# Attention's denominators: the row sums of both query halves in four products of 32 columns, one reciprocal a round, spread over the partitions by ScalarE

## The chip, the cores and the metric

One core of a Trainium2 chip runs the whole program. TensorE (PE in the rows) multiplies, VectorE (DVE), ScalarE (ACT) and GpSimd (POOL) do the rest, and each engine takes its instructions strictly in the order written, waiting on semaphores. The metric is the time of one execution on the device in microseconds. Three runs of the kernel before took 1800.47 to 1801.7 us, median 1801.14.

## The reference

Four layers over x of 4 batches x 1024 tokens x 128 features: attention with 16 heads of 64, experts, a linear attention, experts again, each on a layer norm and added to x. The change is in the first:

```python
s = jnp.einsum('bhid,bhjd->bhij', q * scale, k)
gm = jax.lax.stop_gradient(jnp.max(s, axis=-1, keepdims=True))
p = jnp.where(causal_mask, 0.0, jnp.exp(s - gm))
num = jnp.einsum('bhij,bhjd->bhid', p, v)
out = num / (jnp.sum(p, axis=-1, keepdims=True) + EPS)
```

## The kernel before

Attention takes the first 1245 us. It works in 32 rounds, one for each pair of heads of each batch, and each round has two stages, t = 0 and t = 1. The query rows come in two halves of 512: index n = 0 is the upper half (tokens 512 to 1023, eight parts of keys), n = 1 the lower one (four parts). In round r TensorE makes the scores of round r + 1 (only for their row maxima, which VectorE takes), then the same scores again, turned and shifted by the maximum, for round r. ScalarE exponentiates these tiles into `prob`, POOL masks the diagonal blocks and adds the tiles of a half up into `row_sum[n]`, and TensorE multiplies them by the values into the bank `pv`. Score tiles and shifted tiles share a ring of three banks, so a tile can be written when the one three places before it has been read; `STAGES` writes their order out by hand.

The denominators go through a bank of their own, `alone`, which the turned maxima use too. `sums(p, n)` (L1389 to L1394) multiplies `row_sum[n]` of each head by 64 columns of ones, so each sum stands on all 64 partitions of its head. `denominator` (L1051) copies it out with a small constant added, `inverse` (L1176) takes the reciprocal in two pieces of 128x256 in place, and POOL's `normal` (L935) multiplies the values' product `o[n]` by it. Half n = 0 of round p has its sums at the end of round p, stage 1; half n = 1 has them in stage 0 of round p + 1. The reciprocals of half 0 stand behind VectorE's maxima in stage 0 of round p + 1, those of half 1 in its stage 1; POOL's normalising products follow in stage 1 and in stage 0 of round p + 2.

ScalarE's list at the end of stage 1 is: the tiles, `rows` (the maxima for the next shifts), `high` twice (the next round's projections), then `product_out` (L1046, the copy of `pv`) and `denominator`, and then the next round's tiles. TensorE ends an odd round with `outwards` (L1412), the output projection of two head pairs, which waits for POOL's normalised halves and starts with the rows of half 0; VectorE adds the result to x. In the last round and the two behind it there are no scores for a next round; the first expert weights are split and the first routing is worked out there.

## Time and profile before

| | |
|---|---|
| Median of three runs | 1801.14 us |
| The profiled execution, whole | 1801.88 us |
| Its span | 1800.1 us |
| Busy: PE, DVE, POOL, ACT | 1725.6, 1421.9, 1309.2, 1027.8 us |
| Reciprocals of the denominators (L1179) | 128, 214.7 us busy |
| Copies of the denominators (L1054) | 64, 44.0 us busy |
| Sums' matmuls (L1393), records | 256 |

Busy times are of the whole span. A product of plain 32-bit operands stands as two records in the trace, its two passes. A record's length holds the latency too: the next one starts before it ends, so what a product costs is read from start to start. The trace's span begins and ends with the first and last instruction; 1.8 us lie around it.

### The profile page before, as it was taken

The page shows a single profiled execution, that of the slowest core. Times are in us where ns is not written, and L with a number is a line of the kernel's source. Part 1 is how long each engine was busy: PE and PEld are TensorE (multiplying, and loading weights), DVE is VectorE, ACT ScalarE, POOL GpSimd, SP SyncE. Part 2 cuts the span into 40 slices and gives each one's busy share as a digit, 9 for nine tenths or more (in the row PEclk, how much of TensorE's full clock was granted, in tenths as well). Part 3 has the DMA queues.
Part 4 walks back from the last instruction along what each step waited for, and adds up shares of the span by engine and source line. Part 5 has one row for each costly group of instructions (what it writes and reads, how often), then busy time and mean ns, then how long its engine had stood idle before and what let it go on. Part 6 is the DMA issues. An engine that isn't in the chain of part 4 may idle for free. (4 is left out here: it accounts for less than half of the span.)

```text
span 1800.1 us, 32515 instructions
## 1 busy us (share of the span) xinstructions
PE 1725.6 (96%) x11638; PEld 1263.0 (70%) x11638; DVE 1421.9 (79%) x2459; ACT 1027.8 (57%) x2177; POOL 1309.2 (73%) x1354
## 2 busy tenths in 40 slices
PE   6999999999999999999999999998999979889998
PEld 4767677677776777777777767766888756568786
DVE  6778778787787887777777777765999958979887
ACT  3555444455445444545544445453889876649876
POOL 1777767677686776777667676776899957738998
PEclk9999999999999999999999999998999989989999
DMA  3000000000000000000000000001000000000000
GB/s 95 2 1 1 1 1 1 1 1 1 1 1 2 1 1 1 1 1 1 2 1 1 2 1 1 1 24 32 1 1 1 1 1 1 1 1 7 13 13 18
DMA packets 15088, 10.86 MB, mean 6 GB/s; under 512 B 433, under 2 KB 14546, under 8 KB 14930
## 3 DMA queue, kind: packets, MB, share of 16 engines
q1 hardware_dynamic: 14930, 8.80, 1.7%
q8 instruction: 94, 1.54, 0.3%
q14 instruction: 64, 0.52, 0.1%
HBM read 6.70 MB, written 2.10 MB: 5 GB/s over the span
## 5 line engine op out<-in xcount | busy, mean ns | idle before, releaser
L1160 DVE TENSOR_REDUCE attn_neg<-attn_shared 128x2 f32<-128x1024 f32 x512 | 611.8, 1223 | 250.1 <-PE attn_shared L1340 248.9
L1022 ACT ACTIVATE attn_prob<-attn_shared 128x1024 f32<-128x1024 f32 x288 | 295.1, 1026 | 368.3 <-PE attn_shared L1367 368.2
L924 POOL TENSOR_TENSOR attn_row_sum<-attn_row_sum,attn_prob 128x1024 f32<-128x1024 f32 (+3 forms) x256 | 418.2, 1634 | 24.2
L312 ACT ACTIVATE experts_weighed<-experts_y,kept_gate 128x128 f32<-128x128 f32 x1024 | 278.7, 410 | 50.1 <-PE experts_y L559 42.3
L901 POOL TENSOR_TENSOR attn_prob<-attn_prob,attn_below 128x256 f32<-128x256 f32 x256 | 188.3, 736 | 127.2 <-ACT attn_prob L1022 127.1
L405 DVE SCALAR_TENSOR_TENSOR experts_acc<-experts_y,kept_gate,experts_acc 128x128 f32<-128x128 f32 x896 | 247.2, 342 | 23.0 <-PE experts_y L559 20.6
L919 POOL TENSOR_TENSOR attn_row_sum<-attn_prob 128x1024 f32<-128x1024 f32 x64 | 135.6, 2118 | 162.4 <-ACT attn_prob L1022 159.9
L1336 PE MATMUL attn_shared<-attn_qk_hi 64*128 64x512 f32 x1024 | 232.9, 429 | 8.5 <-DVE attn_qk_lo L1173 2.9
L1340 PE MATMUL attn_shared<-attn_qk_hi,attn_qk_lo 64*128 64x512 f32 x1024 | 215.7, 392 | 0.0
L1179 DVE RECIPROCAL attn_den<-attn_den 128x256 f32<-128x256 f32 x128 | 214.7, 1719 | 0.3 <-ACT attn_den L1054 0.3
L1338 PE MATMUL attn_shared<-attn_qk_lo,attn_qk_hi 64*128 64x512 f32 x1024 | 214.5, 390 | 0.0
L557 PE MATMUL experts_y<-kept_w_hi,kept_xT_hi 128*128 128x512 f32 x512 | 206.0, 402 | 4.0 <-PEq L725 2.1
L558 PE MATMUL experts_y<-kept_w_lo,kept_xT_hi 128*128 128x512 f32 x512 | 202.1, 395 | 0.0
L559 PE MATMUL experts_y<-kept_w_hi,kept_xT_lo 128*128 128x512 f32 x512 | 201.6, 394 | 0.0
L1336 PEld LDWEIGHTS attn_shared<-attn_qk_hi 64*128 64x128 f32 x1024 | 107.4, 184 | 105.2 <-issue 84.8
L233 POOL TENSOR_TENSOR experts_quad_sum<-experts_quad_sum,experts_weighed 128x512 f32<-128x512 f32 x128 | 161.7, 1294 | 4.4 <-ACT experts_weighed L312 4.4
L1049 ACT ACTIVATE attn_o<-attn_pv 128x512 f32<-128x512 f32 x64 | 38.2, 598 | 211.7 <-PE attn_pv L1385 205.8
L1367 PE MATMUL attn_shared<-attn_neg_rows,attn_pick 64*128 64x512 f32 (+3 forms) x768 | 143.5, 344 | 0.0
L1365 PE MATMUL attn_shared<-attn_qk_hi,attn_qk_lo 64*128 64x512 f32 (+3 forms) x768 | 142.8, 342 | 0.0
L1363 PE MATMUL attn_shared<-attn_qk_lo,attn_qk_hi 64*128 64x512 f32 (+3 forms) x768 | 142.3, 342 | 0.0
L1361 PE MATMUL attn_shared<-attn_qk_hi 64*128 64x512 f32 (+3 forms) x768 | 139.7, 335 | 0.0
L1385 PE MATMUL attn_pv<-attn_prob,attn_v 128*64 128x512 f32 (+3 forms) x768 | 134.2, 490 | 2.3 <-POOL attn_prob L901 2.3
(263 smaller groups left out, 3345.3 us busy)
## 6 DMA issues: line engine op xcount, KB each, us to landing
kept_x<-in_L_attn_a_x_dram SPq DMA_DIRECT2D x4, 512.0 KB, 8.6
kept_half_raw<-_ffn_expert_weights_dram SPq DMA_DIRECT2D x4, 512.0 KB, 4.6
out_dram<-kept_x SPq DMA_DIRECT2D x8, 256.0 KB, 2.3
attn_prob<-in_L_attn_a_Wkv_dram SPq DMA_DIRECT2D x2, 512.0 KB, 6.1
attn_prob<-in_L_attn_a_Wq_dram SPq DMA_DIRECT2D x1, 512.0 KB, 4.9
attn_wo<-in_L_attn_a_Wo_dram SPq DMA_DIRECT2D x1, 512.0 KB, 5.7
attn_bo<-in_L_attn_a_bo_dram SPq DMA_DIRECT2D x1, 64.0 KB, 5.8
linear_weights_raw<-in_L_attn_b_Wg_dram SPq DMA_DIRECT2D x1, 64.0 KB
```

What stands on the lines that cost most here:

```text
L312: ins = act.activation(weighed[n][:, e, :], y[fill(pair, quad, odd) % RING][:, e * D:(e + 1) * D], ACT.Copy, scale=k.gate[:, c, quad * PER ...
L405: dve.scalar_tensor_tensor(out=to, in0=y[fill(pair, quad, odd) % RING][:, e * D:(e + 1) * D], scalar=k.gate[:, c, quad * PER + e:quad * PE ...
L557: pe.matmul(y[n % RING][:, :], k.xT_hi[:, at], hi, start=True, stop=False)
L558: pe.matmul(y[n % RING][:, :], k.xT_hi[:, at], lo, start=False, stop=False)
L559: pe.matmul(y[n % RING][:, :], k.xT_lo[:, at], hi, start=False, stop=True).then_inc(mm_ok, 1)
L924: pool.tensor_tensor(row_sum[n][:, :, at:], row_sum[n][:, :, at:], src, ALU.add).then_inc(add_ok, 1)
L1022: act.activation(prob[n % RING][:, :, :], buffer((p, t))[:, :, :], ACT.Exp).then_inc(exp_ok, 1)
L1160: dve.tensor_reduce(neg[p % 2][:, :, b, half], buffer((p, b, half))[:, :, :], AX.X, ALU.max, negate=True).then_inc(max_ok, 1)
L1179: dve.reciprocal(den[n][:, at], den[n][:, at]).then_inc(inv_ok, 1)
L1336: pe.matmul(buffer(u)[:, h, :], hi[head(h), 0, rows], hi[head(h), 1, at], start=True, stop=False)
L1338: pe.matmul(buffer(u)[:, h, :], hi[head(h), 0, rows], lo[head(h), 1, at], start=False, stop=False)
L1340: ins = pe.matmul(buffer(u)[:, h, :], lo[head(h), 0, rows], hi[head(h), 1, at], start=False, stop=True)
```

## The change

The sums of a round are taken once, in stage 0 of the next round: four products of 32 columns of ones, one for each head and half, put the four sums on four quadrants of 32 partitions of `alone`. One `denominator` and one `inverse` of two pieces (in stage 1) serve them all. Then `spread`, on ScalarE in stage 1 ahead of `product_out`, copies the quadrants to where the normalising products need them: four copies of 32x512 into `den[1]`, a wait for them, and two within `den[0]`. POOL's two normalising products both stand in stage 0 of round p + 2. `row_sum` and `o` of half 0 get a second buffer; room for it comes from `qk_lo`, whose second buffer now lies in `k.w_lo`, so the last two splits of expert weights wait for the last shifted tile.

```diff
         if valid(r):
             single.append(("turned", r, 1))
         if valid(r - 1):
-            single.append(("sum", r - 1, 1))
+            single.append(("sum", r - 1, 0))
         if valid(r + 1):
             single.append(("turned", r + 1, 0))
-        if valid(r):
-            single.append(("sum", r, 0))
     place = {u: n for n, u in enumerate(shared)}
     earlier = {u: single[n - 1] if n else None for n, u in enumerate(single)}
 
...
-        qk_lo = [sb(f"qk_lo{i}", [P, 2, N], F32R) for i in range(2)]
+        qk_lo = [sb("qk_lo0", [P, 2, N], F32R), k.w_lo[:, 16:32, :].rearrange("p (m x) d -> p m (x d)", m=2)]
...
-        row_sum = [sb(f"row_sum{n}", [P, 2, HALF]) for n in range(2)]
+        row_sum = [[sb(f"row_sum0_{i}", [P, 2, HALF]) for i in range(2)], [sb("row_sum1", [P, 2, HALF])]]
...
-        o = [sb(f"o{n}", [P, HALF]) for n in range(2)]
+        o = [[sb(f"o0_{i}", [P, HALF]) for i in range(2)], [sb("o1", [P, HALF])]]
...
+        def quadrant(h, n):
+            return slice(QUADRANT * (2 * h + n), QUADRANT * (2 * h + n + 1))
...
                 if i in (0, 8):
-                    need(pool, sum_ok, 2 * (p - 1) + n + 1)
+                    need(pool, sum_ok, p if n else p - 1)
...
 
             def normal(p, n):
 
-                pool.wait_ge(inv_ok, PIECES * (2 * p + n + 1))
+                pool.wait_ge(spread_ok, p + 1)
                 pool.wait_ge(o_ok, 2 * p + n + 1)
                 need(pool, out_ok, (p - 3) // 2 + 1)
-                pool.tensor_tensor(o_norm[p % 3][:, at_half(1 - n)], o[n][:, :], den[n][:, :], ALU.mult).then_inc(norm_ok, 1)
+                pool.tensor_tensor(o_norm[p % 3][:, at_half(1 - n)], product_of(p, n)[:, :], den[n][:, :], ALU.mult).then_inc(norm_ok, 1)
 
             for r in range(FIRST, LAST):
                 for t in range(STEPS):
...
                     if t == 1 and valid(r + 1):
                         cut(r + 1, 0)
                     if t == 0 and valid(r - 2):
+                        normal(r - 2, 0)
                         normal(r - 2, 1)
-                    if t == 1 and valid(r - 1):
-                        normal(r - 1, 0)
                     if (r, t) == (END + 1, 0):
                         pool.wait_ge(first_step, TOPPED)
                         pool.tensor_tensor(weights, weights, wide(top), ALU.subtract).then_inc(first_step, 1)
...
 
             def product_out(p, n):
                 act.wait_ge(pv_ok, UNITS * p + (UNITS if n else 8))
-                need(act, norm_ok, 2 * (p - 1) + n + 1)
-                act.activation(o[n][:, :], pv[:, :], ACT.Copy).then_inc(o_ok, 1)
-
-            def denominator(p, n):
-                act.wait_ge(sum_ok, 2 * p + n + 1)
-                need(act, norm_ok, 2 * (p - 1) + n + 1)
-                act.activation(den[n][:, :], alone[:, :], ACT.Identity, bias=sum_eps[:, :], scale=1.0).then_inc(den_ok, 1)
+                need(act, norm_ok, 2 * p if n else 2 * (p - 2) + 1)
+                act.activation(product_of(p, n)[:, :], pv[:, :], ACT.Copy).then_inc(o_ok, 1)
+
+            def denominator(p):
+                act.wait_ge(sum_ok, p + 1)
+                need(act, norm_ok, 2 * p)
+                act.activation(den[0][:, :], alone[:, :], ACT.Identity, bias=sum_eps[:, :], scale=1.0).then_inc(den_ok, 1)
+
+            def spread(p):
+
+                act.wait_ge(inv_ok, PIECES * (p + 1))
+                for h in range(2):
+                    for n in range(2):
+                        act.activation(den[1][quadrant(h, n), :], den[0][quadrant(h, 1), :], ACT.Copy).then_inc(moved_ok, 1)
+                act.wait_ge(moved_ok, 4 * (p + 1))
+                for h in range(2):
+                    ins = act.activation(den[0][quadrant(h, 1), :], den[0][quadrant(h, 0), :], ACT.Copy)
+                ins.then_inc(spread_ok, 1)
 
             for r in range(FIRST, LAST):
                 for t in range(STEPS):
...
                         if job_at(r, 3) is not None:
                             turned_high(job_at(r, 3))
                         if valid(r - 1):
-                            denominator(r - 1, 1)
+                            denominator(r - 1)
                         if r == END:
                             act.wait_ge(first_step, TURNED_ROUTER)
                             act.activation(k.rT[:, 0, :], router_bank(), ACT.Copy).then_inc(first_step, 1)
...
                         if valid(r + 2):
                             high(r + 2, 0)
                             high(r + 2, 1)
+                        if valid(r - 1):
+                            spread(r - 1)
                         if valid(r):
                             product_out(r, 0)
-                            denominator(r, 0)
                         if r == END:
                             act.wait_ge(first_step, LOGITS)
                             act.activation(weights, first_logits(0), ACT.Copy).then_inc(first_step, 1)
...
                 dve.tensor_tensor(qk_lo[p % 2][:, :, at], buffer(("qk", p, n))[:, :, :], f(qk_hi[p % 2][:, :, at]),
                                   ALU.subtract).then_inc(lo_ok, 1)
 
-            def inverse(p, n, piece):
+            def inverse(p, piece):
                 at = slice(piece * HALF // PIECES, (piece + 1) * HALF // PIECES)
-                dve.wait_ge(den_ok, 2 * p + n + 1)
-                dve.reciprocal(den[n][:, at], den[n][:, at]).then_inc(inv_ok, 1)
+                dve.wait_ge(den_ok, p + 1)
+                dve.reciprocal(den[0][:, at], den[0][:, at]).then_inc(inv_ok, 1)
 
             def into_x(g):
                 c = g // 4 * BLOCKS
...
             def expert_low(q):
                 dve.wait_ge(w_rounded, q + 1)
                 dve.wait_ge(value_ok, ROUNDS)
+                if q >= 2:
+                    dve.wait_ge(shift_ok, len(TILES) * ROUNDS)
                 dve.tensor_tensor(k.w_lo[:, expert_piece(q), :], raw_piece(q), f(k.w_hi[:, expert_piece(q), :]),
                                   ALU.subtract).then_inc(w_split, 1)
 
...
                         maximum(*u)
                     if valid(r + 1):
                         smallest(r + 1, t)
-                    if valid(r - 1):
+                    if t == 1 and valid(r - 1):
                         for piece in range(PIECES):
-                            inverse(r - 1, t, piece)
+                            inverse(r - 1, piece)
                     if t == 0 and job_at(r, 0) is not None:
                         statistics(job_at(r, 0))
                     if t == 1 and job_at(r, 1) is not None:
...
                                     start=(j == 0), stop=(i in (7, 11)))
                 ins.then_inc(pv_ok, 1)
 
-            def sums(p, n):
-                alone_free(("sum", p, n))
-                pe.wait_ge(add_ok, ADDS * p + (11 if n else 7))
+            def sums(p):
+
+                alone_free(("sum", p, 0))
+                pe.wait_ge(add_ok, ADDS * (p + 1))
                 for h in range(2):
-                    ins = pe.matmul(alone[head(h), :], ones[:, :], row_sum[n][:, h, :], start=True, stop=True)
+                    for n in range(2):
+                        ins = pe.matmul(alone[quadrant(h, n), :], ones[:, :], row_sums(p, n)[:, h, :], start=True, stop=True)
                 ins.then_inc(sum_ok, 1)
 
             def turn_router():
...
                 if r == END:
                     turn_router()
                 if valid(r - 1):
-                    sums(r - 1, 1)
+                    sums(r - 1)
                 if valid(r):
                     for i in range(0, 3):
                         product(r, i)
...
                 if valid(r):
                     for i in range(3, 8):
                         product(r, i)
-                    sums(r, 0)
             pe.wait_ge(x_ok, ROUNDS // 2)
 
 
```

`attn_pv` is the bank of the values' product, `attn_alone` that of the sums, `attn_shared` the ring of score tiles. TensorE before, at the end of a round's stage 1:

```order
L1385 MATMUL attn_pv<-attn_prob0,attn_v1 64x256 [waits attn_mask_ok]
L1385 MATMUL attn_pv<-attn_prob0,attn_v1 64x256
L1393 MATMUL attn_alone<-attn_row_sum0,attn_ones 64x512 [waits attn_add_ok,attn_rows_ok]
L1393 MATMUL attn_alone<-attn_row_sum0,attn_ones 64x512
L1336 MATMUL attn_shared0<-attn_qk_hi0 128x512 [waits attn_max_ok,attn_lo_ok]
```

The same place after:

```order
L1406 MATMUL attn_pv<-attn_prob0,attn_v1 64x512 [waits attn_mask_ok]
L1406 MATMUL attn_pv<-attn_prob0,attn_v1 64x512
L1406 MATMUL attn_pv<-attn_prob1,attn_v1 64x256 [waits attn_mask_ok]
L1406 MATMUL attn_pv<-attn_prob1,attn_v1 64x256
L1357 MATMUL attn_shared2<-attn_qk_hi1 128x512 [waits attn_lo_ok]
```

Nothing stands there between the values' product and the scores. TensorE before, stage 0 of a round (values of the next pair, the sums of half 1, the values' product):

```order
L1322 MATMUL attn_shared1<-kept_w_lo,kept_xT_lo 128x256
L1323 MATMUL attn_shared1<-kept_w_lo,kept_xT_hi 128x256
L1393 MATMUL attn_alone<-attn_row_sum1,attn_ones 64x512 [waits attn_add_ok,attn_rows_ok]
L1393 MATMUL attn_alone<-attn_row_sum1,attn_ones 64x512
L1385 MATMUL attn_pv<-attn_prob6,attn_v1 64x512 [waits attn_exp_ok,attn_o_ok,attn_v_ok]
```

The same place after:

```order
L1344 MATMUL attn_shared2<-kept_w_lo,kept_xT_hi 128x256
L1416 MATMUL attn_alone<-attn_row_sum0_0,attn_ones 32x512 [waits attn_add_ok,attn_rows_ok]
L1416 MATMUL attn_alone<-attn_row_sum1,attn_ones 32x512
L1416 MATMUL attn_alone<-attn_row_sum0_0,attn_ones 32x512
L1416 MATMUL attn_alone<-attn_row_sum1,attn_ones 32x512
L1406 MATMUL attn_pv<-attn_prob5,kept_half_raw 64x512 [waits attn_exp_ok,attn_o_ok,attn_v_ok]
```

The two products of 64 columns have become four of 32, and they take both halves' row sums. ScalarE before, the end of stage 1 (maxima, projections, the values' product, the denominator, the next tiles):

```order
L1038 ACTIVATE attn_neg_rows<-attn_alone,attn_own_block 128x128 x4
L1026 ACTIVATE attn_qk_hi<-attn_shared 128x2x512 x2
L1049 ACTIVATE attn_o<-attn_pv 128x512
L1054 ACTIVATE attn_den<-attn_alone,attn_sum_eps 128x512
L1022 ACTIVATE attn_prob<-attn_shared 128x1024 x5
```

And after:

```order
L1045 ACTIVATE attn_neg_rows<-attn_alone,attn_own_block 128x128 x4
L1033 ACTIVATE attn_qk_hi<-attn_shared 128x2x512 x2
L1068 ACTIVATE attn_den<-attn_den 32x512 x4
L1071 ACTIVATE attn_den<-attn_den 32x512 x2
L1056 ACTIVATE attn_o_0<-attn_pv 128x512
L1029 ACTIVATE attn_prob<-attn_shared 128x1024 x5
```

The denominator is gone from there and six copies of `den` stand ahead of the values' product. On POOL the normalising product of half 0 moves from stage 1 to the start of the next stage 0, directly ahead of that of half 1.

## Rows read from the trace of the kernel before

**Rows 1.** table of stretches: us, busy (x instructions) by engine, then TensorE clock

```profile
core 0 of [0], span 1800.1 us
113.15:1168.17 1055.02, 1050.24 (x8170) 750.82 (x8168) 822.56 (x738) 512.93 (x741) 757.50 (x749) 1.00 0.00 1
1206.00:1234.20 28.20, 24.30 (x180) 14.16 (x177) 11.75 (x11) 11.90 (x19) 27.30 (x23) 0.97 0.14 39
```

**Rows 2.** waits, 100 to 1250 us: total us, times, longest

```profile
ACT attn_prob L1022 <- PE attn_shared L1367: 350.2, 266, 3.7
DVE attn_neg L1160 <- PE attn_shared L1340: 235.8, 293, 3.5
PE attn_shared L1336 <- DVE attn_neg L1160: 1.1, 7, 0.2
```

**Rows 3.** timeline of TensorE, end of round 17: start, us, line, names

```profile
708.98 3.73 PE L1423 MATMUL attn_shared<-attn_wo,attn_o_norm 128*128 128x128 f32 x32
715.71 1.03 PE L1393 MATMUL attn_alone<-attn_row_sum,attn_ones 128*64 128x512 f32 x4
```

**Rows 4.** timeline of TensorE, end of round 16 and next stage

```profile
676.37 1.03 PE L1393 MATMUL attn_alone<-attn_row_sum,attn_ones 128*64 128x512 f32 x4
677.33 0.50 PE L1336 MATMUL attn_shared<-attn_qk_hi 64*128 64x512 f32 x2
680.69 0.42 PE L1336 MATMUL attn_shared<-attn_qk_hi 64*128 64x512 f32 x2
```

**Rows 5.** timeline of TensorE's weight loads, sums of stage 0

```profile
617.19 0.20 PEld L1393 LDWEIGHTS attn_alone<-attn_row_sum,attn_ones 128*64 128x64 f32 x4 [0.17 <-issue]
```

**Rows 6.** timeline of VectorE, rounds 16 and 15

```profile
671.76 3.35 DVE L1179 RECIPROCAL attn_den<-attn_den 128x256 f32<-128x256 f32 x2
621.78 1.23 DVE L1160 TENSOR_REDUCE attn_neg<-attn_shared 128x2 f32<-128x1024 f32 x1 [2.16 <-PE attn_shared L1340]
```

**Rows 7.** timeline of ScalarE, 128x512 operations out of SBUF

```profile
1459.14 0.63 ACT L1658 ACTIVATE linear_gate<-linear_raw 128x512 f32<-128x512 f32 x1
1459.81 0.63 ACT L1660 ACTIVATE linear_gate<-linear_gate 128x512 f32<-128x512 f32 x1
1460.34 1.04 ACT L1661 ACTIVATE linear_log<-linear_raw 128x1024 f32<-128x1024 f32 x1
```

**Rows 8.** timeline of ScalarE, ends of rounds 16 and 17

```profile
679.29 1.03 ACT L1022 ACTIVATE attn_prob<-attn_shared 128x1024 f32<-128x1024 f32 x1 [1.15 <-PE attn_shared L1367]
715.92 0.60 ACT L1049 ACTIVATE attn_o<-attn_pv 128x512 f32<-128x512 f32 x1 [5.72 <-PE attn_pv L1385]
```

**Rows 9.** timeline of POOL, start of round 17

```profile
677.35 1.30 POOL L940 TENSOR_TENSOR attn_o_norm<-attn_o,attn_den 128x512 f32<-128x512 f32 x1
682.09 2.40 POOL L919 TENSOR_TENSOR attn_row_sum<-attn_prob 128x1024 f32<-128x1024 f32 x1 [3.45 <-ACT attn_prob L1022]
```

**Rows 10.** timelines of VectorE, POOL and TensorE, rounds 30 to 33

```profile
1199.28 3.35 DVE L1179 RECIPROCAL attn_den<-attn_den 128x256 f32<-128x256 f32 x2
...
1206.10 2.39 POOL L919 TENSOR_TENSOR attn_row_sum<-attn_prob 128x1024 f32<-128x1024 f32 x1
1219.26 1.27 POOL L940 TENSOR_TENSOR attn_o_norm<-attn_o,attn_den 128x512 f32<-128x512 f32 x1
1232.88 1.27 POOL L940 TENSOR_TENSOR attn_o_norm<-attn_o,attn_den 128x512 f32<-128x512 f32 x1
1239.83 1.26 POOL L940 TENSOR_TENSOR attn_o_norm<-attn_o,attn_den 128x512 f32<-128x512 f32 x1 [2.85 <-DVE attn_den L1179]
...
1235.88 3.61 PE L1423 MATMUL attn_shared<-attn_wo,attn_o_norm 128*128 128x128 f32 x16 [0.84 <-POOL attn_o_norm L940]
1241.15 2.05 PE L1423 MATMUL attn_shared<-attn_wo,attn_o_norm 128*128 128x128 f32 x16 [1.66 <-POOL attn_o_norm L940]
```

**Rows 11.** timeline of TensorE, round 15, two score units

```profile
625.33 0.43 PE L1340 MATMUL attn_shared<-attn_qk_hi,attn_qk_lo 64*128 64x512 f32 x2
625.91 0.51 PE L1336 MATMUL attn_shared<-attn_qk_hi 64*128 64x512 f32 x2
```

19 lines of the change are left out of this document (12 added, 7 removed).

## The prediction

> **What bounds the kernel now.** I read the table of stretches first. In the steady part of attention, 1055 of the 1800 us, TensorE is busy 1050.24 us of 1055.02 at full granted clock; VectorE works 822.56, GpSimd 757.50, ScalarE 512.93 us [rows 1]. The waits say the same from the other side: ScalarE spends 350.2 us waiting for the tiles it exponentiates, VectorE 235.8 us for the scores, and TensorE has 1.1 us of idle time put down to VectorE [rows 2]. So a microsecond taken from VectorE is worth nothing by itself, and one taken from TensorE's stream counts, if ScalarE and POOL can follow. After 1206 us this turns over: POOL is busy 27.30 of 28.20 us and TensorE 24.30 [rows 1]. That end is a chain of its own, read row by row at the end of the next part.
>
> Attention is 32 rounds (head pairs) of two stages. Rounds differ by parity: at the end of an odd one TensorE also does a projection outwards (3.73 us [rows 3]), at the end of an even one it does not. The 1055.02 us run from round 1's sums to round 29's, 28 rounds of 37.7 us; I work with round 16 (its sums at 676.37 us) and round 17 (715.71 us) and take the others of a parity for the same.
>
> **The change part by part.**
>
> *TensorE, end of stage 1: a pair of sums goes.* The four records of two products start within 1.03 us less one record's own duration and the scores follow 0.96 us after the first (677.33 - 676.37) [rows 4]. At the full array a record of 128 columns takes 3.73/32 = 0.117 us [rows 3], so four records of 512 columns one after another would stream about 1.8 us; they take 0.96 us with the change of shape to the 64-row scores behind them. So two column groups already work side by side, and the two passes of a product follow each other 0.43 us apart. Streaming is 0.86 us and the change of shape 0.10 us. The sum's 0.86 us goes; the change of shape stays, between the values' product and the scores.
>
> *TensorE, stage 0: two products of 64 columns become four of 32.* No row shows four column groups at once. Lower bound: all four stream together, 0.86 us as now, extra 0. Upper bound: two at a time as now, 1.72 us, extra 0.86 us. I take the lower, because the nearest rows show groups of different columns to be independent to within the resolution of the row, and both passes kept apart: nothing in them is shared but the rows, which are shared already. New beside it is a change of shape between 32 and 64 columns in front of the next values' product; the nearest is the 0.10 us above (bounds 0 and 0.2). So a round gains 0.86 - 0.10 = 0.76 us on TensorE.
>
> What a page would add here: the Trainium skill, "TensorEngine Tiling (Array Packing)", section Tiling Modes, lists four tiles of 128x32 that work independently, which is the lower bound. Against it stands the skill's "TensorE: Matmul & The Clock Gate", section The mechanism: weight loads overlap matmuls in flight only when the row group differs. Here the row group is the same, and the trace disagrees with it for 64 columns: four loads fall within 0.20 us from 617.19 on, while the matmuls that they belong to run for 0.9 us [rows 5]. By that rule the eight loads of a round, 0.14 us each, would stand in the open, 1.1 us a round and some 34 us in all; I keep it inside the first rival with 2 in 100.
>
> *VectorE.* Two reciprocals of 128x256 a round go, 3.35 us [rows 6], 31 times: 104 us of busy time. They stood in stage 0, behind the last maximum; in a round where VectorE had more to do there than usual it still idled 2.16 us before its next score at 621.78 us [rows 6]. That idle time covers them: worth 0. The pair in stage 1 stays where it was, ending at R = 671.76 + 3.35 = 675.11 us in round 16, and with it the low halves behind it.
>
> *ScalarE.* A 128x512 copy with bias goes from the end of stage 1. Six copies of 32x512 come in ahead of the copy of the values' product, and they wait for R. No row has 32 channels. The nearest are 128x512 operations: 0.63 us long, 0.53 us from one start to the next where it is independent (1459.81 to 1460.34), 0.67 us where it waits for the one before (1459.14 to 1459.81) [rows 7]. Lower bound: all at 0.53; upper: every one at 0.67. The program has one such wait, before the fifth copy: three steps of 0.53, one of 0.67, two of 0.53 make 3.32 us until the values' copy starts and about 0.5 us more until the first exponential (the values' copy lasts 0.60 us [rows 8] and overlaps its follower by 0.1, as those do). I add 0.04 us for the wake-up: the first exponential can start at R + 3.86 = 678.97 us.
>
> Even round: the scores now start at 677.33 - 0.86 = 676.47 us, and the third score unit, which takes the buffer that this exponential frees, moves from 680.69 to 679.83 us [rows 4]. The exponential began at 679.29 and ended at 680.32 before [rows 8]; now it ends at 680.00 and is seen a few hundredths later. TensorE stalls about 0.20 us. Later exponentials are spaced by TensorE's 1.63 us and take 1.03 us, so ScalarE catches up at once. Even round: gain 0.76 - 0.20 = 0.56 us. Odd round: ScalarE had idled 5.72 us in front of the values' copy at 715.92 us [rows 8]; 3.4 us of copies fit. Gain 0.76 us.
>
> *POOL.* Its two normalising products now stand together at the start of stage 0 and wait for the spread, which ends at R + 3.5 = 678.6 us; 1.3 us each, so they end at 681.2 us. The first row sum behind them began at 682.09 us after 3.45 us idle; with the 0.86 us gained it is due at 681.2 us, and a stall of ScalarE's moves it back by as much [rows 9]. It just fits; cost 0, and if the cover fails some tenths. The other buffers (second row sum, second product, alias of the low half) remove waits that no row shows: 0.
>
> *Body sum.* Rounds 0 to 29: 16 of them (15 odd ones and round 0, which has no spread yet) by 0.76 = 12.2 us, 14 by 0.56 = 7.8 us: 20.0 us gained.
>
> *The end, from round 30's stage 1.* Reciprocals end at 1199.28 + 3.35 = 1202.63 us. The spread ends 3.5 us later, 1206.1, and two products of 1.3 us bring POOL to 1208.7 us where it began the row sum at 1206.10: 2.6 us late, in the stretch where POOL never rests. The product at 1219.26 moves behind the sums; so the row sums end 1.3 us late, and the two products then end at 1236.8 us against 1234.15 [rows 10]: 2.6 us late. The last sum, its denominator and the reciprocals follow, 2.6 us late: they let POOL's last product go at 1239.83 before, now at 1242.4 us. But there the spread stands in between, to 1245.9 us, and two products behind it, the first to 1247.1. Only then can the outward projection start, of which the first half ran at 1235.88 before, under cover. At full clock its halves take 3.73/2 = 1.87 us and 2.05 us and end at 1251.1 us, against 1243.2: 7.9 us late. The first half ran 3.61 us before, at 1.2 GHz after TensorE had waited on POOL; if both halves do so, the end is about 11 us late. I take 9, between the two. The experts start behind this.
>
> *Total.* The profiled execution took 1801.88 us (span 1800.1 [rows 1] and 1.8 us around it), 0.7 us over the median of the runs. 1801.9 - 20.0 + 9 = 1790.9, and by the median's level 1790.2. I say 1790.5 us.
>
> **Rivals.**
>
> 1. *The four small products run two at a time* (ends on the other side). For it: the trace shows only two groups together. Against: they start as if independent. Price 0.86 us in each of 31 rounds, 26.7 us on TensorE: 1790.5 + 26.7 = 1817 us; half of it (three passes instead of two) gives 1804 us. It turns to slower from 0.46 us a round on. 17 in 100, with the weight-load rule in it.
>
> 2. *ScalarE gives the gain back.* Every copy steps at 0.67 us instead of 0.53, or POOL's pair misses its cover: 5 x 0.14 = 0.7 us more in 14 even rounds, 9.8 us: 1800 us, no change. For it: the slack in even rounds is used up to the last tenth. Against: independent operations overlap [rows 7]. 15 in 100.
>
> 3. *VectorE was a hidden bound.* TensorE's stream has small gaps between score units: from 625.33 to 625.91 us stand 0.58 us where a step of two products takes 0.23 us [rows 11]. If an earlier VectorE closed one such gap of 0.35 us a round, 30 rounds would give 10 us more: 1780 us. Against: VectorE waits before each such stage [rows 6]. 5 in 100. That the 104 us themselves come back is excluded by its 235.8 us of waiting.
>
> **How the numbers follow.** The forecast has 63 in 100. Its own bounds: no stall and no change of shape, 30 x 0.86 = 25.8 us gained less 7.9 at the end, gives 1783 us; a change of shape of 0.2 us, a stall of 0.4 and an end of 11 us give 1799 us. Rivals 1, 2 and 3 have 17, 15 and 5. The range 1783 to 1808 us leaves out the full price of rival 1 (about 12 in 100) and most of rival 3. A measurement here can tell 0.2%, 3.6 us, from no change. Faster: nearly all of the forecast, rival 3 and a little of rival 2, 67 in 100. Same: most of rival 2 and the half price of rival 1, 14. Slower: 19.
>
> **What the profile after would show.** Eight records of the sums within about 1.05 us, once a round (right), or within 1.9 us (rival 1). The copies starting 0.53 us apart, and the first exponential of an even round about 3.9 us after the reciprocals. From the end of round 16's scores stage to the end of round 17's 38.8 us, where 39.34 us stood between their sums [rows 3, 4]. VectorE busy 107 us less with TensorE's busy share in the body unchanged. POOL starting the last row sums 2.6 us after where the round would have them, and the last outward projection in one piece behind two products of POOL. The forecast is wrong if sums take over 1.3 us, if the first exponential stands over 4.5 us behind the reciprocals, or if the end costs less than 6 us or more than 13.

## The result, and the profile after

The changed kernel takes 1806.55 us (median of 8 runs, 1802.2 to 1808.55) beside 1801.18 us of the kernel before on the same chip (8 runs, 1799.7 to 1801.72): a ratio of 1.003, 95% interval 1.0019 to 1.004. It is slower by 0.3% where 0.6% faster was forecast. The range, 1783 to 1808 us, holds the time; the likeliest case does not.

The profiled execution took 1806.37 us, its span 1804.6 us. I read the table of stretches first, from round 1's sums to round 29's, the 28 rounds for which [rows 1] have 1055.02 us. In the changed kernel the sums stand only in stage 0, so the row of before is read again from there. Columns: from:to, us, then busy us (x instructions) of PE, PEld, DVE, ACT and POOL, then TensorE's granted clock, DMA share and GB/s. Before:

```profile
128.94:1183.97 1055.03, 1048.82 (x8157) 749.52 (x8157) 821.54 (x738) 511.39 (x737) 754.89 (x744) 1.00 0.01 1
```

After:

```profile
127.27:1176.64 1049.37, 1031.10 (x8156) 726.87 (x8157) 730.34 (x681) 596.25 (x877) 756.87 (x744) 1.00 0.01 1
```

Three columns did what they should: TensorE 18 us less busy, VectorE 91 us less, ScalarE 85 us more for 168 copies and 28 denominators less. But the 28 rounds are shorter by 5.66 us only, where the forecast had 18.5. TensorE was busy in all but 6.21 us of the stretch before and leaves 18.27 us open now. So the question is what it waits for, and the waits say it (engine line waited for: us in total, times, longest; TensorE, 100 to 1180 us):

```profile
PE attn_shared L1357 <- ACT attn_prob L1029: 11.0, 15, 0.8
PE attn_alone L1416 <- ACT attn_neg_rows L1045: 3.5, 12, 1.6
PE attn_shared L1357 <- DVE attn_neg L1179: 1.8, 11, 0.2
```

The first line is new against [rows 2]: in each of 15 rounds the third score unit waits for an exponential. The place is the end of an even round and the first scores behind it, where [rows 8] have the exponential at 679.29 us (an even round runs, in what follows, from the sums in its stage 0 to those in the next round's). The timelines of VectorE and ScalarE there (start, us, engine, line, names, shape, count, idle time before and who ended it):

```profile
667.49 3.35 DVE L1198 RECIPROCAL attn_den<-attn_den 128x256 f32<-128x256 f32 x2
...
670.88 2.59 ACT L1068 ACTIVATE attn_den<-attn_den 32x512 f32<-32x512 f32 x4 [0.70 <-DVE attn_den L1198]
673.49 1.27 ACT L1071 ACTIVATE attn_den<-attn_den 32x512 f32<-32x512 f32 x2
674.79 0.60 ACT L1056 ACTIVATE attn_o<-attn_pv 128x512 f32<-128x512 f32 x1
675.28 1.94 ACT L1029 ACTIVATE attn_prob<-attn_shared 128x1024 f32<-128x1024 f32 x2
```

and TensorE, which answers to 680.69 of [rows 4]:

```profile
675.32 0.40 PE L1388 MATMUL attn_shared<-attn_neg_rows,attn_pick 64*128 64x512 f32 x2
676.45 0.50 PE L1357 MATMUL attn_shared<-attn_qk_hi 64*128 64x512 f32 x2 [0.73 <-ACT attn_prob L1029]
```

R, the end of the reciprocals, is 667.49 + 3.35 = 670.84 us. The four copies start 0.65 us apart, the sixth is followed by the copy of the values' product (674.79) and this by two exponentials without a gap: ScalarE is late, and the first exponential starts at R + 4.44 us. It was put at R + 3.86. TensorE's step from 675.32 to 676.45 is 1.13 us where its neighbours are 0.23 apart, 0.90 us of waiting.

The sums themselves are fine. TensorE at round 16's sums, which now stand in stage 0 of round 17 (compare 677.33 of [rows 4] and the 715.71 of [rows 3]):

```profile
687.99 1.06 PE L1416 MATMUL attn_alone<-attn_row_sum,attn_ones 128*32 128x512 f32 x8
688.98 0.65 PE L1406 MATMUL attn_pv<-attn_prob,kept_half_raw 128*64 128x512 f32 x2
```

Eight records, four column groups in two passes, in the time in which four stood: the next product follows 0.996 us after the first of them, in every round. Before, the one behind the four records of stage 0 followed after 0.910.

The end, which answers to [rows 10] (POOL, ACT and PE of the last round):

```profile
1228.72 1.07 PE L1416 MATMUL attn_alone<-attn_row_sum,attn_ones 128*32 128x512 f32 x8
1241.77 6.49 PE L1446 MATMUL attn_shared<-attn_wo,attn_o_norm 128*128 128x128 f32 x32 [11.99 <-POOL attn_o_norm L948]
...
1236.41 2.58 ACT L1068 ACTIVATE attn_den<-attn_den 32x512 f32<-32x512 f32 x4 [1.93 <-DVE attn_den L1198]
1239.02 1.27 ACT L1071 ACTIVATE attn_den<-attn_den 32x512 f32<-32x512 f32 x2
...
1240.37 2.49 POOL L948 TENSOR_TENSOR attn_o_norm<-attn_o,attn_den 128x512 f32<-128x512 f32 x2 [6.76 <-ACT attn_den L1071]
```

```profile
1241.80:1248.20 6.40, 6.40 (x32) 6.27 (x32) 0.00 (x0) 0.00 (x0) 1.47 (x2) 0.56 0.00 0
```

TensorE waits 11.99 us, and then the outward projection runs in one piece at a granted clock of 0.56, near the lower of its two levels (1.2 GHz): 6.4 us instead of 3.73 [rows 3].

The budget, in the profiled executions' spans (divided at round 1's and round 29's sums in stage 0 and at the first weight load of the experts):

| piece, us | before | after | difference | forecast |
|---|---|---|---|---|
| up to round 1's sums | 128.94 | 127.27 | -1.7 | -1.5 |
| 28 rounds | 1055.03 | 1049.37 | -5.7 | -18.5 |
| round 29's sums to the experts | 61.27 | 73.42 | +12.2 | +9 |
| the rest | 554.84 | 554.52 | -0.3 | 0 |
| span | 1800.08 | 1804.58 | +4.5 | -11 |

Two terms failed, one by 12.8 us and one by 3.2 us.

### The profile page after: what moved, and what is told of

Its sections match the earlier page's. It is cut to its first block and busy times, and to the rows that moved or that the text cites. A ratio compares the mean times of both kernels' runs of the same rounds, so it can differ in the third digit from the quotient of the medians.

```text
span 1804.6 us, 32546 instructions
## 1 busy us (share of the span) xinstructions
PE 1706.2 (95%) x11638; PEld 1239.5 (69%) x11638; DVE 1317.4 (73%) x2395; ACT 1125.9 (62%) x2337; POOL 1309.5 (73%) x1354
## 5 line engine op out<-in xcount | busy, mean ns | idle before, releaser
L1406 PE MATMUL attn_pv<-attn_prob,kept_half_raw 128*64 128x512 f32 (+3 forms) x768 | 134.4, 492 | 0.0
L948 POOL TENSOR_TENSOR attn_o_norm<-attn_o,attn_den 128x512 f32<-128x512 f32 x64 | 80.8, 1284 | 55.2 <-ACT attn_den L1071 55.2
L557 PEld LDWEIGHTS experts_y<-kept_w_hi,kept_xT_hi 128*128 128x128 f32 x512 | 97.5, 190 | 28.4 <-DVE experts_acc L405 4.3
L559 PEld LDWEIGHTS experts_y<-kept_w_hi,kept_xT_lo 128*128 128x128 f32 x512 | 97.4, 190 | 21.3
L558 PEld LDWEIGHTS experts_y<-kept_w_lo,kept_xT_hi 128*128 128x128 f32 x512 | 97.5, 190 | 18.9
L1056 ACT ACTIVATE attn_o<-attn_pv 128x512 f32<-128x512 f32 x64 | 38.3, 598 | 111.8 <-PE attn_pv L1406 106.9
```

Of the source, the lines that this page charges most:

```text
L557: pe.matmul(y[n % RING][:, :], k.xT_hi[:, at], hi, start=True, stop=False)
L558: pe.matmul(y[n % RING][:, :], k.xT_hi[:, at], lo, start=False, stop=False)
L559: pe.matmul(y[n % RING][:, :], k.xT_lo[:, at], hi, start=False, stop=True).then_inc(mm_ok, 1)
L1406: ins = pe.matmul(pv[head(h), first:], v[g % 2][:, j, cols], slot(p, part)[:, h, place_of(part)], start=(j == 0), stop=(i in (7, 11)))
```

## The experiments

Theory A: ScalarE gives TensorE's gain back; the six copies take longer than the prediction had them, hold the first exponential of the next round, and stand in the chain at the end. Theory B: the 32-column products, or their place, cost TensorE more than they save. Theory C: VectorE or POOL, with their pair of normals, are the ones that are late.

**1. Without the copies.**

```
-                pool.wait_ge(spread_ok, p + 1)
+                pool.wait_ge(inv_ok, PIECES * (p + 1))
...
-                pool.tensor_tensor(o_norm[p % 3][:, at_half(1 - n)], product_of(p, n)[:, :], den[n][:, :], ALU.mult).then_inc(norm_ok, 1)
+                pool.tensor_tensor(o_norm[p % 3][:, at_half(1 - n)], product_of(p, n)[:, :], den[0][:, :], ALU.mult).then_inc(norm_ok, 1)
...
-                        if valid(r - 1):
-                            spread(r - 1)
```

> The changed kernel without the six spreading copies: the normals wait for the reciprocal alone and both halves multiply by the first denominator tile, so the denominators stay unspread and the attention output is another. Everything else stands as in the changed kernel. Theory A (ScalarE gives the gain back): the copies hold the first exponential of the next round until 4.48 us after the products of the sums instead of some 0.6 us, and TensorE waits for it 0.9 us in every even round. Without them the body gives the gain that was forecast (some 13 us more than it gave), and the copies ahead of rounds 30 and 31 go too, 3.9 us each at most: 1806.5 - 13 - 4 to 8 = 1782 to 1790, and the third score unit of even rounds waits less than 0.1 us. Theory B (the 32-column products or their place on TensorE cost more than they save): the copies lie beside other work, the waits before the score units stay, and only the last spread goes from the end: 1802 to 1804. Theory C (the loss is VectorE's or GpSimd's, the two normals side by side): the same as B.

Measured: 1782.52 us (4 runs, 1781.57 to 1784.38), ratio to before 0.9899 [0.9885, 0.9912]. The stretch of 28 rounds:

```profile
126.44:1160.33 1033.89, 1027.81 (x8156) 723.33 (x8156) 730.11 (x681) 492.14 (x709) 754.71 (x744) 1.00 0.01 1
```

1055.03 - 1033.89 = 21.14 us in 28 rounds, 0.755 us a round: the prediction's TensorE term was 0.76. By parity it is 35.73 to 34.97 us in even rounds (those without other work in them, as in all that follows) and 39.30 to 38.56 in odd ones. The wait for the exponential is gone:

```profile
PE attn_alone L1414 <- ACT attn_neg_rows L1045: 1.5, 1, 1.5
PE attn_shared L1355 <- DVE attn_neg L1177: 1.1, 7, 0.2
```

So B is wrong: the products, their shape and their place give all that they were said to. The copies cost 15.5 us in the 28 rounds: 14 x 1.0 us at the ends of even ones, and most of the rest in twelve rounds (nine odd ones of 38.67 us instead of 38.56, three even ones), in which TensorE waits some 0.12 us for ScalarE's rows of maxima (L1045: 3.5 us, 12 times, with the copies, 1.5 us, once, without). At the end 66.40 us stand between round 29's sums and the experts instead of 73.42: the copies are worth 7.0 us there. The other 5.1 us over the 61.27 of before stay without them: no run takes them apart. What is new there is the single sum and reciprocal, behind which both normals stand, and the projection that follows in one piece; without the copies it still takes 6.24 us, after 7.52 us of waiting.

**2 to 4. Fewer copies, and fewer of them ahead.** With five copies, one of 128x512 takes the whole reciprocal over first:

```
+                if step == 0:
+                    act.wait_ge(inv_ok, PIECES * (p + 1))
+                    act.activation(den[1][:, :], den[0][:, :], ACT.Copy).then_inc(moved_ok, 1)
+                    return
+                if step == 1:
+                    act.wait_ge(moved_ok, p + 1)
+                half, h = divmod(step - 1, 2)
+                ins = act.activation(den[half][quadrant(h, 1 - half), :], den[half][quadrant(h, half), :], ACT.Copy)
```

> The same result with five copies instead of six, all ahead of the copy of the values' product: one of 128x512 that takes the whole reciprocal into the second tile, then two of 32x512 in each tile. A normal waits for its own tile. Theory A: one step of 0.65 us goes from ahead of the first exponential, so up to 0.65 us of the 0.9 us stall in each of 14 even rounds (9 us), and the normal of the first half at the end may start two copies sooner: 1795 to 1800. Theories B and C: no change beyond 1 us, 1805 to 1807. The page should show the copies of 32x512 still 0.65 us apart; if a 128x512 copy ahead of them is followed after 0.53 us, it is the width, not the copies' kind, that keeps them from overlapping.

With four ahead, the last copies stand between the next round's exponentials, and POOL's normals behind its first addition:

```
+                    late = list(range(4, 6)) if t == 0 and valid(r - 2) else []
                     for p, i in turned_tiles(r, t):
                         exponential(p, i)
+                        if late:
+                            spread(r - 2, late.pop(0))
...
-                            spread(r - 1)
+                            for step in range(4):
+                                spread(r - 1, step)
```

> The same six copies, but only four of them ahead of the copy of the values' product; the last two follow the first and the second exponential of the next round, and GpSimd's two normals stand behind its first addition of that round instead of at its head. Theory A: the first exponential comes 1.31 us sooner, which is more than the stall of 0.9 us, so even rounds lose nothing there; the copies between the exponentials use time that ScalarE has: 14 x 0.85 = 12 us less, 1793 to 1798. If instead TensorE now waits for the second or third exponential, the gain is under half of it: 1800 to 1804. Theories B and C: 1805 to 1807.

And both together:

> Both edits: five copies, four of them ahead and the last one behind the first exponential, GpSimd's normals behind its first addition. Theory A: the first exponential as in the kernel with four ahead, with one copy of 0.65 us less between the later ones, and the end one or two copies shorter: 1791 to 1797, at or below the fastest of the other two correct ones and below the kernel before (1801). Theories B and C: 1805 to 1807.

Measured, each in 5 runs with the kernel before beside them (1800.49 us):

| kernel | us | ratio to before |
|---|---|---|
| five copies | 1795.47 (1789.43 to 1795.84) | 0.9958 [0.9945, 0.9972] |
| four of six ahead | 1792.89 (1791.76 to 1794.06) | 0.9955 [0.9942, 0.9967] |
| five, four of them ahead | 1790.52 (1787.13 to 1791.98) | 0.994 [0.9928, 0.9953] |

All three are faster than before and than the changed kernel, as A has it and B and C exclude; the last two came out just under the ranges expected (1793 and 1791 us). The 128x512 copy is followed after 0.66 us, but the copy behind it waits for it, so this says nothing on the width. ScalarE with four of six ahead, same place:

```profile
663.00 2.59 ACT L1074 ACTIVATE attn_den<-attn_den 32x512 f32<-32x512 f32 x4 [0.70 <-DVE attn_den L1210]
665.61 0.60 ACT L1059 ACTIVATE attn_o<-attn_pv 128x512 f32<-128x512 f32 x1
666.26 1.03 ACT L1032 ACTIVATE attn_prob<-attn_shared 128x1024 f32<-128x1024 f32 x1
667.32 0.63 ACT L1076 ACTIVATE attn_den<-attn_den 32x512 f32<-32x512 f32 x1
667.96 1.03 ACT L1032 ACTIVATE attn_prob<-attn_shared 128x1024 f32<-128x1024 f32 x1
```

The first exponential starts 3.26 us after the first copy instead of 4.40, and the two late copies cost nothing: the 28 rounds take 1035.43 us, 1.5 over the kernel without any copy. This edit moves POOL's normals too; experiment 8, which leaves them in their place, comes to the same length of the rounds. The one with five copies takes 1039.84 us, the one with both 1035.70.

**5. VectorE's half alone.** In the kernel before:

```
-                pool.wait_ge(inv_ok, PIECES * (2 * p + n + 1))
+                if n:
+                    pool.wait_ge(inv_ok, PIECES * (p + 1))
+                else:
+                    pool.wait_ge(den_ok, 2 * p + 1)
...
-                    if valid(r - 1):
+                    if t == 1 and valid(r - 1):
```

> The kernel before without VectorE's reciprocals of the first half of each round (62 instructions of 3.35 us, the half of VectorE's work that the change takes away): that half is multiplied by its denominator instead, so the output is another. The prediction put VectorE's saving at 0 us, because PE never waits for it in the rounds. By that, within 2 us of the kernel before, 1799 to 1803. By the rival that VectorE was a hidden bound, 7 us faster or more: under 1794.

Measured: 1800.77 us (11 runs) beside 1800.9 us (15 runs), ratio 1.0002 [0.9993, 1.0011]. (It is 64 instructions, 3.35 us a pair.) The stretch of [rows 1], from this kernel's own sums to sums:

```profile
112.05:1166.61 1054.56, 1049.71 (x8171) 746.78 (x8169) 731.21 (x682) 512.88 (x741) 756.97 (x749) 1.00 0.01 1
```

VectorE works 91 us less and the 28 rounds take 1054.56 instead of 1055.02 us, 0.02 us a round. The 104 us were worth nothing that the times show, as forecast, and rival 3, which had 10 us, is excluded.

**6 to 8. Why do the copies not overlap?** The step of 0.53 us in [rows 7] is 0.10 shorter than the operation; the copies' step of 0.65 is 0.02 longer. Three looks at the changed kernel, one run each. One increment for the four copies:

```
-                        act.activation(den[1][quadrant(h, n), :], den[0][quadrant(h, 1), :], ACT.Copy).then_inc(moved_ok, 1)
-                act.wait_ge(moved_ok, 4 * (p + 1))
+                        ins = act.activation(den[1][quadrant(h, n), :], den[0][quadrant(h, 1), :], ACT.Copy)
+                ins.then_inc(moved_ok, 1)
+                act.wait_ge(moved_ok, p + 1)
```

> The changed kernel with one semaphore increment behind the four copies instead of one behind each; the result is the same. Theory A1 (the increment closes the overlap: in the kernel with five copies and four ahead, the one copy without an increment is followed by the copy of the values' product after 0.54 us, where all that carry one take 0.65): the steps after the first three copies fall from 0.654 to about 0.54, the first exponential 0.3 us sooner. Theory A2 (32 partitions, or moving them, takes the overlap away): still 0.64 to 0.655 us.

Each copy to its own partitions:

```
-                        act.activation(den[1][quadrant(h, n), :], den[0][quadrant(h, 1), :], ACT.Copy).then_inc(moved_ok, 1)
+                        act.activation(den[1][quadrant(h, n), :], den[0][quadrant(h, n), :], ACT.Copy).then_inc(moved_ok, 1)
```

> The changed kernel in which the first four copies take each 32 partitions of the reciprocal to the same 32 partitions of the second tile, so nothing is moved across partitions and the second half is divided by other sums. Increments as in the changed kernel. If the move across partitions kept the copies apart, the step falls from 0.654 to about 0.53; if it is the 32 partitions or the increments, it stays at 0.65.

Two copies of 64 partitions for the four of 32:

```
-                    for n in range(2):
-                        act.activation(den[1][quadrant(h, n), :], den[0][quadrant(h, 1), :], ACT.Copy).then_inc(moved_ok, 1)
+                    act.activation(den[1][slice(64 * h, 64 * h + 64), :], den[0][slice(64 - 64 * h, 128 - 64 * h), :], ACT.Copy).then_inc(moved_ok, 1)
```

> The changed kernel in which two copies of 64x512, halves swapped, stand in the place of the first four of 32x512; the second half is divided by other sums. If a copy's time goes by its columns alone, each takes 0.63 us and is followed after 0.65; two steps go (1.3 us), and the first exponential comes at 3.2 us after the first copy instead of 4.4, before TensorE needs it: even rounds as without the spread, 35.0 us instead of 36.0. If a copy of 64 partitions takes longer, the gain is smaller by that.

Measured 1805.75, 1808.32 and 1788.45 us. ScalarE's rows, one kernel after the other:

```profile
671.66 2.55 ACT L1068 ACTIVATE attn_den<-attn_den 32x512 f32<-32x512 f32 x4 [0.70 <-DVE attn_den L1199]
```

```profile
671.73 2.59 ACT L1068 ACTIVATE attn_den<-attn_den 32x512 f32<-32x512 f32 x4 [0.72 <-DVE attn_den L1198]
```

```profile
664.43 1.28 ACT L1067 ACTIVATE attn_den<-attn_den 64x512 f32<-64x512 f32 x2 [0.70 <-DVE attn_den L1197]
665.75 1.27 ACT L1070 ACTIVATE attn_den<-attn_den 32x512 f32<-32x512 f32 x2
```

Four copies in 2.55, 2.59 and (two of them) 1.28 us. The increment is worth 0.013 us a copy (step 0.641 instead of 0.654), the move across partitions nothing, and the number of partitions nothing either: 64 take as long as 32 and as the 128 of experiment 2 (0.63 us). Theory A1, that the increments are the cause, is wrong: they are worth a hundredth, not a tenth. What all these copies share is that each stands next to one of 32 or 64 partitions; experiment 12 takes this up. Two copies fewer ahead do what nothing done to the single one does: the even rounds take 34.97 us, the length without copies, as expected.

**9. Another end** for the kernel with five copies, four ahead: in the last two rounds all ahead, in the last VectorE makes two of them.

```
+                            for step in range(4 if r < END else 5 if r == END else 3):
+                                spread(r - 1, step)
...
+                        if r - 1 == END:
+                            dve.wait_ge(moved_ok, ROUNDS)
+                            for h in range(2):
+                                ins = dve.tensor_copy(den[1][quadrant(h, 0), :], den[1][quadrant(h, 1), :])
+                            ins.then_inc(spread_ok, 1)
```

> The kernel with five copies, four ahead, with another end; the result is the same. In the last two rounds all copies of the reciprocal stand ahead, and in the last one VectorE makes the two copies of the second tile while ScalarE makes those of the first. Theory A: the body is as in that kernel (35.0 and 38.7 us between sums); the end loses one late copy in round 31 and the last normal two copies of 0.65 us: 1 to 2.5 us less, 1788 to 1790. If the end is bound by GpSimd's two normals one behind the other, nothing: 1790 to 1791.

Measured: 1789.48 us (5 runs, 1785.64 to 1790.68), ratio 0.9942 [0.9928, 0.9955] to the 1800.2 us beside it. From round 29's sums to the experts it takes 71.65 us where 72.95 stood: 1.3 us, inside the range expected, but too little to be told apart in the times from the 1790.52 us of the kernel without it. POOL in the last round:

```profile
1224.76 3.47 POOL L948 TENSOR_TENSOR attn_o_norm<-attn_o,attn_den 128x512 f32<-128x512 f32 x2 [4.81 <-ACT attn_den L1075]
```

The two normals stand one behind the other without a gap, so POOL is the next link. The first lasts 1.26 us and the second 2.25, beside VectorE's split of the expert weights; why is not tested.

**10 and 11. The place of the tile, and the kind of the instruction.**

```
-        den = [sb(f"den{n}", [P, HALF]) for n in range(2)]
+        den_first = sb("den0", [P, HALF])
...
+        den = [den_first, sb("den1", [P, HALF])]
```

> The changed kernel with the first denominator tile at another place of the on-chip memory, far from the second. Neither one increment less, nor no move across partitions, nor 64 partitions let the copies overlap; the copy of the values' product overlaps the next instruction by 0.10 us in the kernel before and ends 0.03 us ahead of it in the changed one, where only tiles have moved. If the places of the tiles decide, the steps of 0.654 us change here to about 0.53; if not, they stay.

```
-                        act.activation(den[1][quadrant(h, n), :], den[0][quadrant(h, 1), :], ACT.Copy).then_inc(moved_ok, 1)
+                        act.activation(den[1][quadrant(h, n), :], den[0][quadrant(h, 1), :], ACT.Identity,
+                                       bias=sum_eps[quadrant(h, n), :], scale=1.0).then_inc(moved_ok, 1)
```

> The changed kernel whose first four copies are an Identity with a bias tile and a scale, as the rows with 0.09 us overlap from on-chip memory are (the gate's), instead of a Copy; the second half's reciprocals get a small constant more. If the kind of the instruction decides, the step falls from 0.654 to 0.53; otherwise it stays at 0.65.

Measured 1806.51 and 1812.69 us, one run each. With the tile elsewhere:

```profile
671.11 2.58 ACT L1069 ACTIVATE attn_den<-attn_den 32x512 f32<-32x512 f32 x4 [0.70 <-DVE attn_den L1199]
```

With the Identity:

```profile
675.08 2.95 ACT L1068 ACTIVATE attn_den<-attn_den,attn_sum_eps 32x512 f32<-32x512 f32 x4 [0.72 <-DVE attn_den L1199]
679.85 1.93 ACT L1029 ACTIVATE attn_prob<-attn_shared 128x1024 f32<-128x1024 f32 x2
```

Neither overlaps. The Identity takes 0.720 us instead of 0.629 for its bias tile and steps at 0.745. That makes it a second dose of the suspected cost, upwards, beside the first, downwards. All kernels in one table (medians over the even rounds; of the length, over the shortest group of them, into which no other work and no late row of maxima falls):

| kernel | first copy to first exponential, us | even round, us |
|---|---|---|
| no copies | | 34.97 |
| four of six ahead | 3.27 | 34.93 |
| two of 64 and two of 32 | 3.27 | 34.97 |
| five copies | 3.75 | 35.27 |
| one increment | 4.37 | 35.92 |
| changed kernel | 4.41 | 35.95 |
| Identity | 4.78 | 36.32 |

From 3.75 us on the round grows by as much as the exponential is late: 1.03 us later, 1.05 us longer. The line meets 34.97 at 3.45 us. Part of this is a fixed price of waiting at all: TensorE's score unit behind the wait takes 1.70 us to the next one, and 1.62 without a wait. The slack itself can be read without the copies, where the third unit starts unhindered (R is 658.85 + 3.35 = 662.20 us there):

```profile
658.85 3.35 DVE L1196 RECIPROCAL attn_den<-attn_den 128x256 f32<-128x256 f32 x2
```

```profile
666.68 0.40 PE L1386 MATMUL attn_shared<-attn_neg_rows,attn_pick 64*128 64x512 f32 x2
666.92 0.40 PE L1355 MATMUL attn_shared<-attn_qk_hi 64*128 64x512 f32 x2
```

It is due at R + 4.72, the exponential lasts 1.03 us and TensorE follows its end by 0.14, so it may start at R + 3.55, 3.5 us after the first copy. This settles theory A for the even rounds: what they lose is the lateness of one exponential, whatever makes it.

**12. Full width.** What was left was the width. An observation pointed to it: in the changed kernel the copy of the values' product overlaps the rows behind it (L1056, L1045) by 0.10 us in 12 rounds only, those where a table was loaded or the gate's rows ran since the copies, and starts them 0.025 us after its end in the other 19. Without the copies all 31 overlap.

```
-                for h in range(2):
-                    for n in range(2):
-                        act.activation(den[1][quadrant(h, n), :], den[0][quadrant(h, 1), :], ACT.Copy).then_inc(moved_ok, 1)
-                act.wait_ge(moved_ok, 4 * (p + 1))
-                for h in range(2):
-                    ins = act.activation(den[0][quadrant(h, 1), :], den[0][quadrant(h, 0), :], ACT.Copy)
+                for c in range(2):
+                    ins = act.activation(den[1][:, c * P * 2:(c + 1) * P * 2], den[0][:, c * P * 2:(c + 1) * P * 2], ACT.Copy)
```

> The changed kernel with two copies of 128x256 in the place of all six, each taking half of the reciprocal's columns to the same partitions of the second tile; the denominators stay unspread. All copies so far had one of 32 or 64 partitions as a neighbour. And in the changed kernel the copy of the values' product overlaps the rows behind it by 0.10 us in 12 rounds, those in which another function's table was loaded or the gate's rows ran since the copies, and in 19 it does not; without the copies it does in all 31. Theory A3 (an instruction on fewer than 128 partitions takes the overlap away, and for later pairs too): here the second copy starts some 0.32 us after the first (0.19 + 256 columns at 0.87 ns = 0.41 us long, less 0.10), and all 31 pairs overlap. Theory A4 (the copy from on-chip memory itself does it): the second starts after 0.43 us, and again 19 pairs do not. Either way the first exponential is early enough and the time near 1783 to 1786 us.

Measured: 1779.27 us, one run, 4 us under the range expected. The 28 rounds take 1033.96 us, as without copies; what is less lies behind attention, where nothing was changed: 549.9 us instead of the 554.2 of the kernel without copies. The first 8 us of the experts there, with copies of full width and then without copies:

```profile
1227.58:1235.58 8.00, 7.94 (x37) 6.25 (x38) 3.81 (x15) 4.53 (x19) 1.96 (x9) 1.00 0.15 41
```

```profile
1226.73:1234.73 8.00, 7.97 (x25) 6.67 (x26) 1.77 (x7) 2.94 (x12) 1.23 (x7) 0.57 0.15 41
```

The granted clock was 1.00 in one and 0.57 in the other. It was 0.57 in the kernel before and in the changed one, and 1.00 in the profiled runs of experiments 5, 8 and 9. A single time can differ by this much with nothing changed, so the readings here rest on the rounds' lengths. ScalarE, and what TensorE waits for in the rounds:

```profile
662.67 0.72 ACT L1067 ACTIVATE attn_den<-attn_den 128x256 f32<-128x256 f32 x2 [0.70 <-DVE attn_den L1194]
```

```profile
PE attn_alone L1412 <- ACT attn_neg_rows L1045: 1.5, 1, 1.5
PE attn_shared L1353 <- DVE attn_neg L1175: 1.1, 7, 0.2
```

The two copies start 0.323 us apart and last 0.417 and 0.402: an overlap of 0.094 us, the 0.10 of [rows 7], in all 32 rounds, for the same kind of instruction, tiles and memory as in the changed kernel. They also have 256 columns instead of 512, and the first has no increment; but [rows 7] overlap at 512 columns, and in experiment 6 the 32x512 copies without an increment did not overlap. All 31 copies of the values' product overlap their rows again, and all 14 odd rounds take 38.51 to 38.59 us, as without copies, where at least nine of them have 38.6 to 38.75 in every kernel with narrow copies. So it is the width, as theory A3 had it for the copies: in no kernel here does a copy of 32 or 64 partitions overlap another one.

On the instructions behind them the traces say more than A3. At the end of round 16 in the changed kernel the copy of the values' product (674.79, 0.60 long) stands directly behind the narrow copies, and the exponential starts at 675.28, before its end. Earlier in that round, 14 us after the last narrow copy (636.07), the same copy and the rows of maxima do not overlap:

```profile
650.22 0.60 ACT L1056 ACTIVATE attn_o<-attn_pv 128x512 f32<-128x512 f32 x1 [3.46 <-PE attn_pv L1406]
650.85 1.14 ACT L1045 ACTIVATE attn_neg_rows<-attn_alone,attn_own_block 128x128 fp32r<-128x128 f32 x4
```

The rows take a tile as their scale (`own_block`); the exponentials and plain copies take no tile as scale or bias. In attention the first full-width instruction with such a tile behind narrow copies starts 0.024 to 0.027 us after the end of the one before it in all 26 places where it follows at once (19 times the rows, 6 times the gate's rows, once the denominator), and the plain ones ahead of it, 33 of them exponentials, overlap the one before them in all 34. The same 26 stand apart in every kernel with narrow copies. In the 12 rounds that overlap, another such instruction had run in between: the gate's rows, or the square root behind the table's load, whose bias is a tile. That costs the twelve rounds their 0.12 us: the rows of maxima come 0.13 us later, and TensorE waits for them.

## Why the prediction was wrong, by its steps

- *TensorE, 0.86 - 0.10 = 0.76 us a round.* Right: 0.755 without the copies. The change of shape is in the step to the next product, 0.996 us instead of 0.910, 0.09 where 0.10 was put. Four column groups go side by side, in both passes: the starts of the eight records lie at 0, 0.006, 0.013, 0.020 and 0.453, 0.460, 0.466, 0.473 us. Rival 1 did not come, nor the weight loads in the open. By the Trainium skill ("TensorEngine Tiling (Array Packing)", section Key Properties) tiles of the array work independently; the trace agrees for 128x32.
- *VectorE, 104 us worth 0.* Right, and shown alone (ratio 1.0002, 0.02 us a round).
- *POOL's pair fits.* Right, and as narrowly as it was put. Behind the end of round 16 POOL's rows in the changed kernel are

```profile
674.84 2.53 POOL L948 TENSOR_TENSOR attn_o_norm<-attn_o,attn_den 128x512 f32<-128x512 f32 x2 [1.70 <-ACT attn_den L1071]
677.36 2.40 POOL L927 TENSOR_TENSOR attn_row_sum<-attn_prob 128x1024 f32<-128x1024 f32 x1
```

  The row sum starts as the pair ends, and 0.14 us after the end of the second exponential (677.22), which is the delay that it has behind an exponential without a pair in its way. In the kernels with five copies and with copies of 64 partitions, where the pair stands at the same place, POOL is idle for 0.8 to 1.3 us behind it.
- *ScalarE: three steps of 0.53, one of 0.67, two of 0.53, a stall of 0.20 us.* **This is the step that failed.** The prediction took the overlap of independent 128x512 operations [rows 7] for the copies of 32 partitions, with 0.67 as the upper bound, and put the whole of the upper bound into rival 2. Measured are steps of 0.654, 0.654, 0.651, 0.659, 0.644 and 0.651 us. That puts the first exponential at R + 4.44 instead of R + 3.86: 0.58 us. The slack was read right (the third unit is due at R + 4.72, as forecast), but TensorE followed the exponential's end by 0.14 us, not by a few hundredths, and the unit behind the wait took 0.08 us longer. 0.20 + 0.58 + 0.11 + 0.08 = 0.97 us a round, 14 times, is 10.8 us more than forecast. The 0.12 us of twelve rounds, 1.4 us, stood in no term; they come from the rows of maxima behind the narrow copies (experiment 12). That is 12.2 of the 12.8 us. Rival 2 named this mechanism and priced it at 9.8 us: it is what happened.
- *The end, 9 us, between 7.9 and 11.* Found 12.2. Up to the last sums it was 3.0 us late (2.6 forecast). Behind them, 9.2 instead of 6.4: the whole projection ran at the lower clock after TensorE had waited 12 us. That case stood in the working as the 11 us; it was the one to take, since the wait before it was going to grow from 0.84 us [rows 10] to over ten. The spread was 0.4 us longer than put (3.9 us, 1236.41 to 1240.29), by the same step.
- *The sum.* Two of the four terms were right to 0.1 us a round and are worth 21 us. The two that failed add 16 us: 12.8 in the rounds by the length of ScalarE's copies and what hangs on it, 3.2 at the end, mostly by the lower clock. 1790.5 + 16 = 1806.5.
- *The signs of being wrong.* None of the three was reached: the sums took 1.06 us (limit 1.3), the first exponential stood at R + 4.44 (4.5), the end cost 12.2 us (13). With a slack that ended at R + 3.55, a limit of 4.5 allowed a stall of nearly a microsecond in every even round, which is more than the gain.

The Trainium skill, "ScalarE: Activation LUTs", section What ACT_TABLE_LOAD costs, says that each pointer operand adds about 93 ns and that ACTIVATEs one behind the other overlap by about 93 ns. On the first the trace agrees (0.720 against 0.629 us for the bias tile). On the second it agrees at 128 partitions (0.094 us in experiment 12) and not between copies of 32 or 64, where the next starts 0.012 to 0.025 us after the end. By that rule alone the first exponential would have come at about R + 3.9, an estimate, and the same as the prediction's.

What stays open: one narrow copy did overlap a full-width one. In the kernels with five copies, four ahead, the third of the 32x512 copies, without an increment, is followed by the copy of the values' product after 0.54 us in the 16 rounds where that is ready, while a late 32x512 copy without an increment is followed by an exponential 0.012 us after its end in all 30 places of experiment 3. And that it is the tile of scale or bias behind which the overlap returns is read from which rounds have it, not tried.

## What to carry to other kernels

Where an engine takes over work in front of the instruction that frees the bottleneck's buffer, count the steps at the rows' longest until an instruction of that very shape has been seen to overlap: six bets of 0.1 us each were laid here on a gain of 0.76. Set the limit for being wrong where the gain would be gone. Then look whether all of the work must stand ahead: four instead of six copies ahead turned 0.3% slower into 0.45% faster, with the same work. And an instruction on 32 partitions costs what one on 128 does, so the first question is how few of them there can be.

## What the runs showed of the hardware

- ScalarE's overlap of neighbouring copies depends on their partitions: 128x256 ones start 0.323 us apart at 0.417 us of length; 32x512 and 64x512 ones start 0.654 apart at 0.629 (32x512 without an increment 0.641).
- Copies of 32x512, 64x512 and 128x512 f32 all last 0.63 us.
- Behind narrow copies the first full-width instruction with a tile as scale or bias does not overlap the one before it (26 of 26 places, 0.025 us apart, 0.10 us of overlap without the narrow copies); plain ones before it do (34 of 34).
- A score unit of TensorE behind a wait of 0.2 to 1.3 us took 1.70 us to the next, and 1.62 us without a wait.
- The step from the sums to a product of 64 columns was 0.996 us behind eight records of 32 columns and 0.910 behind four of 64.
- The lower clock at the end: after 12 us of waiting, 32 products of 128x128 took 6.4 us at a granted clock of 0.56, against 3.73 us at 1.00. The first 8 us of the experts ran at 0.57 in some profiled runs and at 1.00 in others.
